# Ternary weights at the end of the first stage: the second matrix on DVE, the first on Pool

## The chip, the cores and the metric

The kernel runs on one core of a Trainium2 chip. The metric is the device time of one execution in microseconds (us). Of several runs the median is taken.

## What is computed

The reference takes `x` of 8 sequences of 512 tokens with 128 features and adds eight blocks to it in turn: a slot attention, a mixture of low-rank experts, an attention with polar positions, the experts again, a distance attention, a ternary feed-forward block, a gated attention, and the same feed-forward block again. The change touches how the two weight matrices of the feed-forward block are made. In the reference:

```
def _bitlinear(x, w_latent):
    scale = clip(mean(abs(w_latent), axis=1, keepdims=True), 1e-05, None)
    tern = clip(round(w_latent / scale), -1.0, 1.0)
    w = w_latent + (tern - w_latent)
    return x @ (w * scale).T
h = _bitlinear(x, w_fc) + gate * (x @ v.T @ fast_b.T @ u.T)
r = maximum(h, 0.0)
return _bitlinear(r * r, w_proj)
```

`w_fc` is 512x128 and `w_proj` is 128x512, both f32.

## The kernel before

The program has three groups, each a block of instruction streams for the engines, with a barrier between them: `slot_phase` (the first stage: the slot attention), `middle_group` and `last_group`. All waits between engines and within one are semaphores written by hand. Each engine's stream is the order in which the code calls the methods.

The first stage is a software pipeline over the 8 sequences b. Step s works on sequence s in its first part, s - 1 in its second, s - 2 in its third and s - 3 in the last (`batch(s, n)` gives the sequence, or none). There are 11 steps (0 to 10). In step LAST = 9 only sequence 7's third part and sequence 6's last part are left, and in step 10 sequence 7's last part. Into these two steps the class `FoldWeights` puts the preparation of weights for the later stages:

- `absolute_sums` (DVE) sums the absolute values of the rows of both matrices and signals `sums_ready`.
- `ternary(pool, i)`, i = 0 for the first matrix (fc, viewed as 4 blocks of 128x128 with a scale each) and i = 1 for the second (proj, one block of 128x512): three operations on the scales, comparisons with half the scale and its negative (lines 2293 and 2295, one for each block), a subtraction, an add and a subtraction on 128x512 (lines 2297 to 2299), and a multiply with the scale for each block (line 2301). `then_wait` makes the engine wait until an instruction of its own has finished. It works in the tiles that the trace calls `s_rzk` (fc) and `s_zk` (proj) and in `s_kT`, buffer 0. Pool does both at the end of its stream, the first matrix first, and signals `ternary_ready` after each.
- `turn_ternary(pe, i)` (line 2369) turns the four 128x128 blocks into PSUM bank 0 (fc) or 2 (proj). PE does fc in step LAST, behind `mean_squares` of sequence 7, and proj at the end of its stream, behind `project_out` of sequence 7.
- `finish_fc` (DVE, line 2375) adds the low-rank part and writes `sv.ffn1_fc`. It stands in step LAST, behind the add of sequence 6, and ahead of `apply_rms` of sequence 7. `finish_proj` (ACT, line 2379) copies the turned proj to `sv.ffn1_proj` at the end of ACT's stream.

The end of sequence 7's own work is: `mean_squares` (PE, L2177), `inverse_rms` (ACT, L2182 and L2184), `apply_rms` (DVE, L2189), `apply_gate` (DVE, L2195), `project_out` (PE, L2201, eight matmul instructions) and `add` (DVE, L2207). In the middle of the pipeline Pool's `rope` (L1884, L1889, L1890) runs beside DVE's `scan` (L1984).

Of the kernel before, what the change touches and what calls it, by code (L numbers as in the profile page):

```python
# [10 lines left out]
ALU = mybir.AluOpType  # L11
# [2198 lines left out]
class FoldWeights:  # L2210
# [4 lines left out]
    def __init__(self, nc, sv, tag, slot):  # L2215
# [15 lines left out]
        self.loaded, self.turned, self.copied, self.folded, self.kept, self.multiplied, self.products_kept, self.sums_ready, self.ternary_ready, self.ternary_turned, self.step = [  # L2231
            nc.alloc_semaphore(f"{tag}_{n}") for n in
            ("loaded", "turned", "copied", "folded", "kept", "multiplied", "products_kept", "sums_ready", "ternary_ready", "ternary_turned", "step")]
        self.steps = 0
# [37 lines left out]
    def then_wait(self, pool, instruction):  # L2272
        self.steps += 1
        instruction.then_inc(self.step, 1)
        pool.wait_ge(self.step, self.steps)
# [9 lines left out]
    def ternary(self, pool, i):  # L2285
        view, to, scale = self.raws()[i], (self.fc, self.proj)[i], self.scale[i]
        whole, low = [t.rearrange("p (k c) -> p k c", k=view.shape[1]) for t in (to, self.slot.kT[0][:, :])]
        pool.wait_ge(self.sums_ready, 2)
        self.then_wait(pool, pool.tensor_scalar(scale[1], scale[0], 1.0 / view.shape[2], 1e-5, ALU.mult, ALU.max))
        pool.tensor_scalar(scale[2], scale[1], 0.5, None, ALU.mult)  # L2290
        self.then_wait(pool, pool.tensor_scalar(scale[3], scale[1], -0.5, None, ALU.mult))
        for k in range(view.shape[1]):
            pool.tensor_scalar(whole[:, k, :], view[:, k, :], scale[2][:, k:k + 1], None, ALU.is_gt)
        for k in range(view.shape[1]):
            last = pool.tensor_scalar(low[:, k, :], view[:, k, :], scale[3][:, k:k + 1], None, ALU.is_lt)
        self.then_wait(pool, last)
        self.then_wait(pool, pool.tensor_tensor(whole, low, whole, ALU.subtract))
        self.then_wait(pool, pool.tensor_tensor(whole, whole, view, ALU.add))
        self.then_wait(pool, pool.tensor_tensor(whole, view, whole, ALU.subtract))
        for k in range(view.shape[1]):  # L2300
            last = pool.tensor_scalar(whole[:, k, :], whole[:, k, :], scale[1][:, k:k + 1], None, ALU.mult)
        last.then_inc(self.ternary_ready, 1)
# [62 lines left out]
    def turn_ternary(self, pe, i):  # L2365
        pe.wait_ge(self.ternary_ready, i + 1)
        pe.wait_ge(self.slot.a_ready[2 * i], NB)
        for k in range(NK):
            last = pe.transpose(self.banks.tensors[2 * i][:, k * P:(k + 1) * P], (self.fc, self.proj)[i][:, k * P:(k + 1) * P], self.sv.ident[:, :])
        last.then_inc(self.ternary_turned, 1)  # L2370

    def finish_fc(self, dve):
        dve.wait_ge(self.ternary_turned, 1)
        dve.wait_ge(self.products_kept, 2)
        dve.tensor_tensor(self.sv.ffn1_fc[:, :], self.banks.tensors[0][:, :], self.lowrank, ALU.add)

    def finish_proj(self, act):
        act.wait_ge(self.ternary_turned, 2)
# [3 lines left out]
def slot_phase(nc, sv, tag, a):  # L2382
# [3 lines left out]
    with nc.cleanup_on_exit():  # L2386
# [32 lines left out]
        with nc.Block() as block:  # L2419
# [16 lines left out]
            def _(pe):  # L2436
                pe.wait_ge(constants, ALL_CONSTANTS)
                pe.wait_ge(memsets, 3)
                for s in STEPS:
# [42 lines left out]
                    if s == LAST:  # L2482
                        folding.turn_ternary(pe, 0)
# [10 lines left out]
                folding.turn_ternary(pe, 1)  # L2494
# [55 lines left out]
            def _(dve):  # L2550
                slot.set_up_rows(dve)
                for s in STEPS:
# [44 lines left out]
                    if s == LAST:  # L2597
                        slot.add(dve, LAST - 3)
                        folding.finish_fc(dve)
# [10 lines left out]
                    for b in batch(s, 2):  # L2610
                        slot.apply_gate(dve, b)

            @block.gpsimd
            def _(pool):
# [18 lines left out]
                for i in range(2):  # L2633
                    folding.ternary(pool, i)
# [349 lines left out]
```

## Time and profile before

| | |
|---|---|
| runs | 1858.34, 1852.22, 1856.51 us: median 1856.51 |
| profiled execution | 1852.65 us |
| its span | 1850.9 us |
| mean granted clock of TensorE | 0.932 of full |
| busy share of PE, DVE, ACT, POOL | 87%, 66%, 70%, 20% |
| end of the first stage | about 312 us from the span's start |

The profile is of one execution. PE is TensorE's matmul, PEld its weight load, DVE is VectorE, ACT is ScalarE, POOL is GpSimd. A line number such as L2301 is that of the kernel. A tile is given with its name in the program, without its buffer number. The idle time in brackets at the end of a row is that of the engine ahead of the instruction, and behind the arrow is what ended it.

### The profile page before, as it was taken

The numbers are of one execution on the slowest core, as the hardware profiler recorded it, in microseconds if no ns is written. First come the engines' busy times: TensorE is split into PE (matmuls) and PEld (weight loads), VectorE is DVE, ScalarE is ACT, GpSimd is POOL, SyncE is SP. The second block draws the span as 40 slices with busy tenths as digits, with TensorE's granted clock in tenths as the row PEclk, the third lists the DMA queues.
The fourth block names the chain that finished last, engine by engine and source line by source line (L and its number), as shares of the span: only waits on it lengthen the run. The fifth ranks groups of instructions, "written<-read, shape, count | busy, mean of one in ns | idle before, by whom it ended". The sixth has DMA issues, their size and how long they took to land. (4 is left out here: it accounts for less than half of the span.)

```text
span 1850.9 us, 39127 instructions
## 1 busy us (share of the span) xinstructions
PE 1610.0 (87%) x14558; PEld 773.2 (42%) x14558; DVE 1227.3 (66%) x2494; ACT 1296.8 (70%) x2201; POOL 376.0 (20%) x669
## 2 busy tenths in 40 slices
PE   7999994865999999976789999777766999999988
PEld 4676763641233333345523333344441333333356
DVE  4777775798899999946410000136658999999833
ACT  4646543883788888855569999757763888888863
POOL 3423325641000000014200000023330000000153
PEclk9999896985999999998889999999975999999999
DMA  4000000055222222200132111001233222222101
GB/s 122 1 1 1 1 1 1 1 171 167 57 79 79 71 72 80 59 1 10 35 95 59 56 56 56 11 18 54 73 100 102 57 64 60 56 61 63 30 7 41
DMA packets 115392, 98.51 MB, mean 53 GB/s; under 512 B 26762, under 2 KB 105412, under 8 KB 115204
## 3 DMA queue, kind: packets, MB, share of 16 engines
q1 hardware_dynamic: 114148, 95.68, 18.2%
q8 instruction: 117, 1.92, 0.4%
q14 instruction: 71, 0.58, 0.1%
q10 hardware_dynamic: 1056, 0.33, 0.1%
HBM read 63.82 MB, written 31.59 MB: 52 GB/s over the span
## 5 line engine op out<-in xcount | busy, mean ns | idle before, releaser
L1613 ACT ACTIVATE m_probs<-m_psum 128x512 f32<-128x512 f32 (+1 forms) x768 | 513.8, 758 | 101.8 <-PE m_psum L1530 96.6
L1613 ACT ACTIVATE e_probs<-e_psum 128x512 f32<-128x512 f32 x512 | 277.2, 597 | 84.6 <-PE e_psum L1530 79.0
L1658 DVE TENSOR_REDUCE a_minus_max<-m_psum 128x1 f32<-128x512 f32 x512 | 316.2, 683 | 18.0 <-PE m_psum L1539 15.1
L1658 DVE TENSOR_REDUCE a_minus_max<-e_psum 128x1 f32<-128x512 f32 x512 | 316.1, 682 | 13.1 <-PE e_psum L1539 8.3
L1530 PE MATMUL m_psum<-m_q_stack,m_k_stack 114*32 114x512 bf16 (+1 forms) x4096 | 295.7, 385 | 17.4 <-DMA m_k_stack<-n_parts 8.4
L1550 PE MATMUL m_psum<-m_probs,m_v_ones 128*32 128x512 f32 x2048 | 270.9, 601 | 2.3 <-ACT m_probs L1613 1.6
L1530 PEld LDWEIGHTS m_psum<-m_q_stack,m_k_stack 114*32 114x32 bf16 (+1 forms) x4096 | 102.2, 96 | 222.3 <-issue 126.7
L1530 PE MATMUL e_psum<-e_q_stack,e_k_stack 126*32 126x512 bf16 x2048 | 158.5, 385 | 4.6 <-issue 2.5
L1502 POOL CAST a_max_parts<-a_minus_max 128x16 bf16<-128x16 f32 x64 | 12.6, 196 | 656.3 <-DVE a_minus_max L1658 656.3
L1550 PE MATMUL e_psum<-e_probs,e_v_ones 128*32 128x512 f32 x1024 | 133.3, 595 | 0.9 <-ACT e_probs L1613 0.8
L1539 PE MATMUL m_psum<-m_k_stack,m_q_stack 48*128 48x512 bf16 x512 | 113.4, 399 | 16.9 <-DVE a_minus_max L1658 16.7
L1603 DVE COPY m_ctxT<-m_psum 128x512 f32<-128x512 f32 x16 | 11.1, 691 | 176.4 <-PE m_psum L1550 176.4
L1539 PE MATMUL e_psum<-e_k_stack,e_q_stack 60*128 60x512 bf16 x512 | 113.4, 399 | 15.5 <-DVE a_minus_max L1658 15.3
L1530 PEld LDWEIGHTS e_psum<-e_q_stack,e_k_stack 126*32 126x32 bf16 x2048 | 43.4, 95 | 110.0 <-ACT e_probs L1613 61.7
L1550 PEld LDWEIGHTS m_psum<-m_probs,m_v_ones 128*32 128x32 f32 x2048 | 51.8, 110 | 69.0 <-ACT m_probs L1613 45.8
L1539 PEld LDWEIGHTS m_psum<-m_k_stack,m_q_stack 48*128 48x128 bf16 x512 | 29.4, 94 | 115.3 <-DVE a_minus_max L1658 86.2
L1539 PEld LDWEIGHTS e_psum<-e_k_stack,e_q_stack 60*128 60x128 bf16 x512 | 29.6, 94 | 114.8 <-DVE a_minus_max L1658 87.1
L1884 POOL TENSOR_TENSOR s_rope_product<-s_qkv,rope 128x512 f32<-128x512 f32 x32 | 40.3, 1288 | 156.4 <-ACT s_qkv L1849 156.4
L1495 POOL COPY m_v_ones<-vtok 128x128 f32<-128x128 f32 x64 | 18.6, 291 | 245.2 <-PE m_psum L1550 245.2
L254 ACT ACTIVATE e_q_stack<-x,e_v_ones 128x128 f32<-128x128 f32 x64 | 26.3, 482 | 36.2 <-POOL e_v_ones L247 36.2
L1669 DVE RECIPROCAL m_inv<-m_psum 128x32 f32<-128x32 f32 x32 | 11.3, 353 | 59.2 <-PE m_psum L1558 59.2
L2172 ACT ACTIVATE s_o<-s_bank 128x512 f32<-128x512 f32 x8 | 4.8, 597 | 58.0 <-PE s_bank L2165 58.0
(427 smaller groups left out, 2758.7 us busy)
## 6 DMA issues: line engine op xcount, KB each, us to landing
polar_q<-m_late SPq DMA_DIRECT2D x24, 256.0 KB, 3.0
polar_k<-m_late SPq DMA_DIRECT2D x24, 256.0 KB, 3.1
m_q_stack<-polar_q SPq DMA_DIRECT2D x64, 96.0 KB, 2.3
m_k_stack<-polar_k SPq DMA_DIRECT2D x64, 96.0 KB, 2.3
m_q_stack<-dist_parts SPq DMA_DIRECT2D x192, 32.0 KB
m_k_stack<-dist_parts SPq DMA_DIRECT2D x192, 32.0 KB
gate_parts<-e_late SPq DMA_DIRECT2D x24, 256.0 KB, 3.0
e_q_stack<-gate_parts SPq DMA_DIRECT2D x64, 72.0 KB
```

Of the source, the lines that this page charges most:

```text
L254: last = act.activation(self.xn[:, u, t, :], self.sv.x[:, b * NT + t, :], ACT.Identity, bias=self.shift[:, u, t:t + 1], scale=self.rstd[:, ...
L1495: pool.tensor_copy(self.buf.v_ones[n % 2][:, :, :, 16 * (n % 2):16 * (n % 2) + DH], self.sv.vtok[:, tiles_of(b), g * GW:(g + 1) * GW].rear ...
L1502: pool.tensor_copy(self.max_parts[:, 0, :], self.minus_max[n % 2][:, :]).then_inc(self.hi_ready, 1)
L1530: last = pe.matmul(self.ps_s[i % self.PAIRS][r:r + 32, j, :], self.buf.k_stack[g][0:self.rows, h, c * P + r:c * P + r + 32], self.buf.q_st ...
L1539: pe.matmul(to[:, :], self.buf.q_stack[g][part, h, t * P:(t + 1) * P], self.buf.k_stack[g][part, h, :], start=True, stop=True).then_inc(se ...
L1550: last = pe.matmul(self.ps_pv[32 * h:32 * h + self.buf.VW, :], self.buf.v_ones[m % 2][:, c, h, :], self.buf.probs[(NT * m + c) % self.buf. ...
L1603: copied = eng.tensor_copy(self.buf.ctxT[m // 2 % 2][:, :], self.ps_pv[:, :])
L1613: act.activation(self.buf.probs[(NT * m + c) % self.buf.PROBS][:, self.WIDE * part:self.WIDE * (part + 1), :], self.ps_s[i % self.PAIRS], ...
L1658: dve.tensor_reduce(self.minus_max[n % 2][:, k:k + 1], ps[:, :], AX.X, ALU.max, negate=True).then_inc(self.bank_free, 1)
L1669: dve.reciprocal(inv[:, :, :, :], raw[:, :, :, :, DH]).then_inc(self.inv_ready, 1)
L1884: pool.tensor_tensor(self.products[n][:, :, :, :], halves[:, :, :, i, :], table, ALU.mult).then_inc(self.rope_steps, 1)
L2172: act.activation(self.o2[b % 2][:, :], self.banks.of("o")[:, :], ACT.Square).then_inc(self.o2_ready, 1)
```

## The change

The work of the two ternary matrices is split over two engines. `ternary(dve, 1)` stands in DVE's stream where `finish_fc` was, in step LAST behind the add of sequence 6. Pool does `ternary(pool, 0)` alone. PE turns proj in step LAST and fc at the end of its stream. `finish_fc` goes to the end of DVE's stream. The semaphores `ternary_ready`, `ternary_turned` and `step` become one for each matrix, and the comparison's tile is `kT` buffer 0 for fc and 1 for proj.

```diff
--- before.py
+++ after.py
@@ -2228,10 +2228,11 @@
             spare[0][0:R, 0:HID], spare[0][0:R, HID:HID + D], spare[0][0:R, HID + D:HID + D + R], spare[0][:, 672:672 + D], spare[0][:, 800:800 + D])
         self.woT, self.lowrank = spare[1][:, 0:D], spare[1][:, D:D + HID]
         self.slot = slot
-        self.loaded, self.turned, self.copied, self.folded, self.kept, self.multiplied, self.products_kept, self.sums_ready, self.ternary_ready, self.ternary_turned, self.step = [
+        self.loaded, self.turned, self.copied, self.folded, self.kept, self.multiplied, self.products_kept, self.sums_ready = [
             nc.alloc_semaphore(f"{tag}_{n}") for n in
-            ("loaded", "turned", "copied", "folded", "kept", "multiplied", "products_kept", "sums_ready", "ternary_ready", "ternary_turned", "step")]
-        self.steps = 0
+            ("loaded", "turned", "copied", "folded", "kept", "multiplied", "products_kept", "sums_ready")]
+        self.ternary_ready, self.ternary_turned, self.step = [[nc.alloc_semaphore(f"{tag}_{n}{i}") for i in range(2)] for n in ("ternary_ready", "ternary_turned", "step")]
+        self.steps = [0, 0]
 
     def loads(self, a):
         sv, out = self.sv, []
@@ -2269,10 +2270,10 @@
         self.all_loaded = 16 * len(out)
         return out
 
-    def then_wait(self, pool, instruction):
-        self.steps += 1
-        instruction.then_inc(self.step, 1)
-        pool.wait_ge(self.step, self.steps)
+    def then_wait(self, eng, i, instruction):
+        self.steps[i] += 1
+        instruction.then_inc(self.step[i], 1)
+        eng.wait_ge(self.step[i], self.steps[i])
 
     def raws(self):
         return (self.sv.ffn1_fc[:, :].rearrange("p (k c) -> p k c", k=NK), self.sv.ffn1_proj[:, :, :].rearrange("p k c -> p (k c)").unsqueeze(1))
@@ -2282,24 +2283,24 @@
         for view, scale in zip(self.raws(), self.scale):
             dve.tensor_reduce(scale[0], view, AX.X, ALU.add, apply_absolute_value=True).then_inc(self.sums_ready, 1)
 
-    def ternary(self, pool, i):
+    def ternary(self, eng, i):
         view, to, scale = self.raws()[i], (self.fc, self.proj)[i], self.scale[i]
-        whole, low = [t.rearrange("p (k c) -> p k c", k=view.shape[1]) for t in (to, self.slot.kT[0][:, :])]
-        pool.wait_ge(self.sums_ready, 2)
-        self.then_wait(pool, pool.tensor_scalar(scale[1], scale[0], 1.0 / view.shape[2], 1e-5, ALU.mult, ALU.max))
-        pool.tensor_scalar(scale[2], scale[1], 0.5, None, ALU.mult)
-        self.then_wait(pool, pool.tensor_scalar(scale[3], scale[1], -0.5, None, ALU.mult))
+        whole, low = [t.rearrange("p (k c) -> p k c", k=view.shape[1]) for t in (to, self.slot.kT[i][:, :])]
+        eng.wait_ge(self.sums_ready, 2)
+        self.then_wait(eng, i, eng.tensor_scalar(scale[1], scale[0], 1.0 / view.shape[2], 1e-5, ALU.mult, ALU.max))
+        eng.tensor_scalar(scale[2], scale[1], 0.5, None, ALU.mult)
+        self.then_wait(eng, i, eng.tensor_scalar(scale[3], scale[1], -0.5, None, ALU.mult))
         for k in range(view.shape[1]):
-            pool.tensor_scalar(whole[:, k, :], view[:, k, :], scale[2][:, k:k + 1], None, ALU.is_gt)
+            eng.tensor_scalar(whole[:, k, :], view[:, k, :], scale[2][:, k:k + 1], None, ALU.is_gt)
         for k in range(view.shape[1]):
-            last = pool.tensor_scalar(low[:, k, :], view[:, k, :], scale[3][:, k:k + 1], None, ALU.is_lt)
-        self.then_wait(pool, last)
-        self.then_wait(pool, pool.tensor_tensor(whole, low, whole, ALU.subtract))
-        self.then_wait(pool, pool.tensor_tensor(whole, whole, view, ALU.add))
-        self.then_wait(pool, pool.tensor_tensor(whole, view, whole, ALU.subtract))
+            last = eng.tensor_scalar(low[:, k, :], view[:, k, :], scale[3][:, k:k + 1], None, ALU.is_lt)
+        self.then_wait(eng, i, last)
+        self.then_wait(eng, i, eng.tensor_tensor(whole, low, whole, ALU.subtract))
+        self.then_wait(eng, i, eng.tensor_tensor(whole, whole, view, ALU.add))
+        self.then_wait(eng, i, eng.tensor_tensor(whole, view, whole, ALU.subtract))
         for k in range(view.shape[1]):
-            last = pool.tensor_scalar(whole[:, k, :], whole[:, k, :], scale[1][:, k:k + 1], None, ALU.mult)
-        last.then_inc(self.ternary_ready, 1)
+            last = eng.tensor_scalar(whole[:, k, :], whole[:, k, :], scale[1][:, k:k + 1], None, ALU.mult)
+        last.then_inc(self.ternary_ready[i], 1)
 
     def turn(self, pe):
         sv, ident, bank, slot = self.sv, self.sv.ident, self.banks.tensors, self.slot
@@ -2363,19 +2364,19 @@
         act.activation(self.lowrank, bank[7][:, :], ACT.Copy, scale=sv.gate[:, 0:1]).then_inc(self.products_kept, 1)
 
     def turn_ternary(self, pe, i):
-        pe.wait_ge(self.ternary_ready, i + 1)
+        pe.wait_ge(self.ternary_ready[i], 1)
         pe.wait_ge(self.slot.a_ready[2 * i], NB)
         for k in range(NK):
             last = pe.transpose(self.banks.tensors[2 * i][:, k * P:(k + 1) * P], (self.fc, self.proj)[i][:, k * P:(k + 1) * P], self.sv.ident[:, :])
-        last.then_inc(self.ternary_turned, 1)
+        last.then_inc(self.ternary_turned[i], 1)
 
     def finish_fc(self, dve):
-        dve.wait_ge(self.ternary_turned, 1)
+        dve.wait_ge(self.ternary_turned[0], 1)
         dve.wait_ge(self.products_kept, 2)
         dve.tensor_tensor(self.sv.ffn1_fc[:, :], self.banks.tensors[0][:, :], self.lowrank, ALU.add)
 
     def finish_proj(self, act):
-        act.wait_ge(self.ternary_turned, 2)
+        act.wait_ge(self.ternary_turned[1], 1)
         act.activation(self.sv.ffn1_proj[:, :, :], self.banks.tensors[2][:, :].rearrange("p (k d) -> p k d", k=NK), ACT.Copy)
 
 
@@ -2480,7 +2481,7 @@
                     for b in batch(s, 2):
                         slot.mean_squares(pe, b)
                     if s == LAST:
-                        folding.turn_ternary(pe, 0)
+                        folding.turn_ternary(pe, 1)
                     else:
                         for b in batch(s, 3):
                             slot.project_out(pe, b)
@@ -2491,7 +2492,7 @@
                         slot.gate(pe, b)
                         slot.slot(pe, b, 1)
                         slot.slot(pe, b, 0)
-                folding.turn_ternary(pe, 1)
+                folding.turn_ternary(pe, 0)
 
             @block.scalar
             def _(act):
@@ -2596,7 +2597,7 @@
                         slot.mask_attention(dve, b, 3)
                     if s == LAST:
                         slot.add(dve, LAST - 3)
-                        folding.finish_fc(dve)
+                        folding.ternary(dve, 1)
                     for b in batch(s, 1):
                         slot.scale_logits(dve, b, 0)
                         slot.maximum(dve, b)
@@ -2609,6 +2610,7 @@
                             slot.add(dve, b)
                     for b in batch(s, 2):
                         slot.apply_gate(dve, b)
+                folding.finish_fc(dve)
 
             @block.gpsimd
             def _(pool):
@@ -2630,8 +2632,7 @@
                         slot.sum_three(pool, b)
                     for b in batch(s + 1, 0):
                         slot.rope(pool, b)
-                for i in range(2):
-                    folding.ternary(pool, i)
+                folding.ternary(pool, 0)
 
 
 _INS = []
```

## Rows read from the trace of the kernel before

**Rows 1.** The page's head.

```profile
span 1850.9 us, 39127 instructions
```

**Rows 2.** Order of time, 288 to 315 us: start, duration, engine, line, operation, tiles, idle time.

```profile
288.25 0.24 POOL L2289 TENSOR_SCALAR s_rzk<-s_rzk 128x4 f32<-128x4 f32 x1 [30.59 <-DVE s_zk L2283]
...
294.14 0.68 DVE L2207 TENSOR_TENSOR x<-s_bank,x 128x512 f32<-128x512 f32 x1
...
295.24 1.27 POOL L2298 TENSOR_TENSOR s_rzk<-s_rzk,ffn_fc 128x512 f32<-128x512 f32 x1
...
297.95 2.36 POOL L2301 TENSOR_SCALAR s_rzk<-s_rzk 128x128 f32<-128x128 f32 x4
...
299.04 0.63 ACT L2184 ACTIVATE s_o<-s_o 128x512 f32<-128x512 f32 x1
...
300.37 1.08 PE L2369 MATMUL s_bank<-ident,s_rzk 128*128 128x128 f32 x4 [2.08 <-POOL s_rzk L2301]
...
301.49 0.69 DVE L2375 TENSOR_TENSOR ffn_fc<-s_bank,s_qk 128x512 f32<-128x512 f32 x1 [6.67 <-PE s_bank L2369]
...
302.10 0.68 DVE L2189 TENSOR_TENSOR s_og<-s_bank,s_o 128x512 f32<-128x512 f32 x1
...
302.81 0.69 DVE L2195 TENSOR_TENSOR s_og<-s_og,s_sig 128x512 f32<-128x512 f32 x1
...
303.56 2.08 PE L2201 MATMUL s_bank<-slot_wo,s_og 128*128 128x128 f32 x8 [2.10 <-DVE s_og L2195]
...
305.67 0.69 DVE L2207 TENSOR_TENSOR x<-s_bank,x 128x512 f32<-128x512 f32 x1 [2.17 <-PE s_bank L2201]
...
308.99 1.57 POOL L2301 TENSOR_SCALAR s_zk<-s_zk 128x512 f32<-128x512 f32 x1
...
310.62 1.11 PE L2369 MATMUL s_bank<-ident,s_zk 128*128 128x128 f32 x4 [4.99 <-POOL s_zk L2301]
...
311.77 0.60 ACT L2379 ACTIVATE ffn_proj<-s_bank 128x512 f32<-128x512 f32 x1 [12.10 <-PE s_bank L2369]
...
314.26 0.87 DVE L228 BATCH_NORM_STATS2 m_ctxT<-x 128x6 f32<-128x128 f32 x4 [7.90 <-PEq L2386]
```

**Rows 3.** The view of waits, 284 to 315 us: total, times, longest.

```profile
DVE ffn_fc L2375 <- PE s_bank L2369: 6.7, 1, 6.7
```

**Rows 4.** DVE's instructions of two lines (ns min/median/max), and a group of the page.

```profile
L568 DVE TENSOR_SCALAR m_late<-pope_table,m_late x1: 481/481/481, 317.4 to 317.4; 128x512 f32<-128x512 f32 x1
...
L559 DVE TENSOR_SCALAR m_late<-m_late x1: 153/153/153, 315.6 to 315.6; 128x1 f32<-128x1 f32 x1
...
L1905 DVE TENSOR_SCALAR vtok<-s_bank 128x512 f32<-128x512 f32 x32 | 21.7, 681 | 20.1 <-PE s_bank L1895 20.1
```

**Rows 5.** Order of time, 217.5 to 221.2 us; L1984's instructions (ns min/median/max).

```profile
217.57 1.27 POOL L1889 TENSOR_TENSOR s_qk<-s_rope_product 128x512 f32<-128x512 f32 x1
...
217.78 2.14 DVE L1984 TENSOR_TENSOR_SCAN s_zvT<-ones,s_wvT 128x512 f32<-128x512 f32 x1
...
218.81 2.18 POOL L1890 TENSOR_TENSOR s_qk<-s_rope_product 128x512 f32<-128x512 f32 x1
...
L1984 DVE TENSOR_TENSOR_SCAN s_zvT<-ones,s_wvT x16: 1212/1224/2167, 42.1 to 280.3; 128x512 f32<-128x512 f32 x16
```

**Rows 6.** Order of time at 302.77; L2290's instructions (ns min/median/max).

```profile
302.77 2.10 POOL L2295 TENSOR_SCALAR s_kT<-ffn_proj,s_zk 128x512 f32<-128x512 f32 x1
...
L2290 POOL TENSOR_SCALAR s_rzk<-s_rzk x1: 405/405/405, 288.6 to 288.6; 128x4 f32<-128x4 f32 x1
...
L2290 POOL TENSOR_SCALAR s_zk<-s_zk x1: 211/211/211, 300.7 to 300.7; 128x1 f32<-128x1 f32 x1
```

**Rows 7.** Busy time by stretch: PE, PEld, DVE, ACT, POOL, PEclk, DMA share, GB/s.

```profile
300.00:302.00 2.00, 1.08 (x4) 0.68 (x4) 0.51 (x1) 0.00 (x0) 1.73 (x5) 0.61 0.00 0
302.00:326.00 24.00, 7.99 (x33) 6.80 (x34) 11.68 (x58) 8.01 (x17) 14.80 (x21) 0.50 0.00 1
326.00:328.00 2.00, 2.00 (x13) 2.00 (x13) 1.63 (x9) 1.59 (x5) 1.92 (x4) 0.56 0.00 0
```

## The prediction

> **What bounds the kernel now.** I read the page first: 1850.9 us of span on one core [rows 1]. The change touches only the end of the first stage, so I went to the order of time there and looked for what ends last [rows 2]. The stage ends at a barrier, and the next stage's first DVE instruction comes at 314.26. Three chains run into that barrier. Pool makes the ternary weights of the first matrix (fc) from 288.25 to 300.31 (297.95 plus 2.36), then those of the second (proj) until 310.56 (308.99 plus 1.57). PE turns proj from 310.62 to 311.73 and ACT copies it from 311.77 to 312.37: this is the last work of the stage. The second chain is sequence 7 through DVE and PE (`apply_rms`, `apply_gate`, `project_out`, `add`), which ends at 306.36 (305.67 plus 0.69). The third, `finish_fc`, is in the middle of the second: DVE has waited 6.67 us for it and starts it at 301.49. The view of waits says the same of DVE: 6.7 us for fc [rows 3]; ACT has waited 12.10 us for proj [rows 2]. So the stage's end is set by Pool's serial 22.3 us, and DVE has idle time from 294.82 to 301.49. From ACT's end to the next stage's first DVE instruction is 1.89 us, which I leave as it is.
>
> **What the change does to each chain.** Nothing before 294.82 moves: the sums that both need are ready at 288.2, and DVE reaches the place of `ternary(dve, 1)` with the end of the add of sequence 6 (294.14 plus 0.68). Pool's queue loses proj (10.25 us, 310.56 less 300.31) and nothing is queued behind it. The transposes and ACT's copy of proj keep their size, only their time changes. No DMA is issued or moved.
>
> DVE's new work is nine instructions: three on one column, two comparisons, three two-input operations and one multiply, each on 128x512 f32. The nearest DVE rows: 0.153 us for a column [rows 4], 0.48 for a tensor_scalar from SBUF to SBUF (0.48 is the row; the same form from PSUM takes 0.68, and I keep that as the upper bound), 0.69 for a two-input operation with both inputs in SBUF (302.81) [rows 2, 4]. Alone that is 0.5 + 3 x 0.48 + 3 x 0.69 plus some 0.04 per dependency, about 4.2 us, so DVE would be ready at 299.1; with the upper bound for the tensor_scalars, at 299.7.
>
> But it isn't alone, because Pool is at fc at the same time. The trace shows that the two exclude each other. A DVE scan with two SBUF inputs began at 217.78, 0.21 us into a Pool operation that ran to 218.84, and took 2.14 us, where its like takes 1.22; it ended at 219.92, 1.08 after Pool's end. Pool's next operation began at 218.81 and took 2.18 instead of 1.27; it ended at 220.99, 1.07 after DVE's end [rows 5]. So each waited for the other's whole operation, and turns were taken. From this an operation holds the common resource for its time less 0.14 (DVE) or 0.20 (Pool). Pool's proj comparison shows it again: 2.10 us where the like multiply takes 1.57 [rows 2, 6], with DVE's 0.69 us two-input operation in it: 0.53 lost, as 0.69 less 0.14 would have it. For DVE's tensor_scalar the witness is Pool's four-column operation that took 405 ns beside it and 211 ns otherwise [rows 6].
>
> The Trainium skill, SBUF — State Buffer, section Who interferes with whom, says that DVE in a two-port mode, or with two SBUF inputs, and a GpSimd operation lock each other out for the whole instruction, and that the one that issues first wins. By that rule this change puts two engines on one port and would give little beyond taking turns; the trace agrees where it shows it (2.14 us against 1.22). Without any lock the sum would be the 7.5 us below.
>
> The walk by turns, from 294.8. DVE's three columns are done and its first comparison begins at about 295.2, as Pool's subtraction ends; it holds to 295.5. Pool's add (295.24 in the trace) then holds 1.07, to 296.6; DVE's second comparison to 296.8; Pool's second subtraction to 297.9; DVE's subtraction (0.54) to 298.45; then Pool's four multiplies, 0.40 of hold each, alternate with DVE's add (0.54), subtraction (0.54) and multiply (0.27): 298.85, 299.4, 299.8, 300.3, 300.7, 301.0, and Pool's last to 301.4. So DVE has proj at about 301.1 (2.0 later than alone) and Pool has fc at 301.5 (1.2 later than 300.31).
>
> From there: ACT's inverse rms has been ready since 299.67 (299.04 plus 0.63), so `apply_rms` starts at 301.1 in place of 302.10, `apply_gate` at 301.85 in place of 302.81, and PE starts `project_out` at 302.6 in place of 303.56. PE turns proj before that: 1.08 us from 301.2 to 302.3, in the gap; ACT copies it by 303.0. What is queued behind PE's wait for DVE's proj is `project_out` alone, and its own input comes later from the same DVE queue, so that wait costs nothing. `project_out` ends at 304.7 (2.08). Behind it PE turns fc, which has been ready since 301.5: four transposes at the low clock's 0.22 each, to 305.55. DVE adds sequence 7 from 304.7 to 305.4, then `finish_fc` (0.69) from 305.6 to 306.3. That is the new end: 312.37 less 306.3, **6.1 us less**. What is late next is no longer Pool but DVE's and PE's chain of sequence 7, with the turn of fc and `finish_fc` appended (0.9 us).
>
> `finish_fc` moved to the end costs 0.9 there; in its old place it held up sequence 7 by 6.67 us. The three more semaphores and the barrier I price at nothing: their cover is the 1.89 us between stages; were it gone, some tenths.
>
> **Rivals.**
> *Pool wins every turn.* Its steps follow each other within 0.1 us, so DVE might get in only when Pool is through. Then fc is ready at 300.6, DVE does a subtraction, an add, a subtraction and the multiply after it (0.54 + 0.72 + 0.72 + 0.5, about 2.5) and is at `apply_rms` at 303.1, 1.0 later than in the trace; `project_out` runs 304.6 to 306.7, the turn of fc to 307.5, the end is 308.2. Gain 4.2 us, 0.23%. For it: the back-to-back Pool steps. Against: the scan did get in between two of them [rows 5].
> *No contention worth the name.* DVE is ready at 299.1 to 299.7 and waits for the rms (299.67); `project_out` 301.1 to 303.2, fc turned by 304.1, end 304.9. Gain 7.5 us, 0.40%. Against it the same rows. If instead DVE wins every turn, it is through at 299.1, Pool at about 303.8, fc is turned by 304.9 and the end is 305.7: 6.7 us, near my own.
> *The gain is given back later.* The next stage starts 6 us earlier against PE's clock, which fell at 301 (0.61 in 300 to 302) and rose at 327 (0.56 in 326 to 328) [rows 7]. If it rises no earlier than now, 6 us more of that stage's PE work is done at 1.2 GHz. Those 6 us hold at most 3 us of PE work at full speed that would take 6, and DVE and ACT share the path, so I estimate 1 to 3 us given back, leaving 3 to 5: within 0.3%.
> *Slower.* The same clock is the mechanism: the place is the second stage's head, the price is one us for each us of fully busy PE work that falls from 2.4 to 1.2 GHz. The sign turns at 6.1 us of such work, and slower by 0.3% (5.6 us) needs 11.7 us of it. Between 326 and 328 PE is fully busy, so it isn't impossible, but from 302 to 326 PE is busy 7.99 of 24 us [rows 7], a third, so it would take a far longer low stretch to hold 11.7 us of PE work. Time: 1862.
> *The change doesn't do what it says*, that is, DVE's ternary isn't started in its idle time: it can't be late, as its inputs are ready 6 us before.
>
> **How the numbers follow.** The sum is made against the profiled execution: 1850.9 of span and 1852.65 in all, so 1844.8 and 1846.6 there; the median of the runs shown is 1856.51, 3.9 above the profiled one, and the same 6.1 us from it give 1850.4 (0.33%). Chances: turns taken, or DVE first (6.1 to 6.7 us), 0.45; Pool first 0.15; no contention 0.15; part given back 0.19; slower 0.06. A measurement of this kernel can tell about 0.3% (5.6 us) from nothing; the three runs lie 6.1 us apart. My forecast stands just past that bound, so two thirds of its chance count as faster, with nine tenths of no contention and some tenth of the others: 0.48. Slower 0.06, within 0.3% the rest, 0.46. The range: no contention gives 1849, Pool first 1852, given back 1851.5 to 1853.5; with the scatter of a median of such runs, 2 to 3 us each way, 1846 to 1857.
>
> **What the profile after would show.** DVE's nine instructions from 294.8 to about 301, some with 1.3 to 1.6 us where 0.69 is normal; Pool's steps of fc stretched likewise and done at 301 to 302; `project_out` of sequence 7 at about 302.6; DVE's `finish_fc` last, at about 305.6 to 306.3; the next stage's first DVE instruction at about 308.2. Wrong would be: a comparison on DVE well over 0.68 with Pool idle; Pool's fc later than 304.7, when it, and no longer sequence 7, would set the end; a barrier longer than 1.9 us; or the rest of the kernel taking over 1 us more than its present 1536.6 us from 314.26 to the end.

## The result and the profile after

The change makes the kernel a little faster, by 0.38%. Over 20 runs each, the median goes from 1855.20 us (1851.39 to 1863.30) to 1847.71 us (1844.27 to 1856.48); the ratio is 0.9962, with a 95% interval of 0.9947 to 0.9976, which is 4.4 to 9.8 us. The forecast was 1850.4 in a range of 1846 to 1857, and 6.1 us of gain. The profiled execution takes 1846.34 us, its span is 1844.6, 6.3 less than before.

Order of time at the end of the changed kernel's first stage, the counterpart of [rows 2]:

```profile
289.25 0.24 POOL L2290 TENSOR_SCALAR s_rzk<-s_rzk 128x4 f32<-128x4 f32 x1 [30.59 <-DVE s_zk L2284]
...
295.05 0.68 DVE L2207 TENSOR_TENSOR x<-s_bank,x 128x512 f32<-128x512 f32 x1
...
295.89 0.14 DVE L2292 TENSOR_SCALAR s_zk<-s_zk 128x1 f32<-128x1 f32 x1
...
296.07 0.48 DVE L2294 TENSOR_SCALAR s_zk<-ffn_proj,s_zk 128x512 f32<-128x512 f32 x1
...
296.25 1.43 POOL L2299 TENSOR_TENSOR s_rzk<-s_rzk,ffn_fc 128x512 f32<-128x512 f32 x1
...
296.47 1.50 DVE L2296 TENSOR_SCALAR s_kT<-ffn_proj,s_zk 128x512 f32<-128x512 f32 x1
...
297.76 1.33 POOL L2300 TENSOR_TENSOR s_rzk<-ffn_fc,s_rzk 128x512 f32<-128x512 f32 x1
...
298.00 1.64 DVE L2298 TENSOR_TENSOR s_zk<-s_kT,s_zk 128x512 f32<-128x512 f32 x1
...
299.19 3.24 POOL L2302 TENSOR_SCALAR s_rzk<-s_rzk 128x128 f32<-128x128 f32 x4
...
299.67 0.74 DVE L2299 TENSOR_TENSOR s_zk<-s_zk,ffn_proj 128x512 f32<-128x512 f32 x1
...
299.94 0.63 ACT L2184 ACTIVATE s_o<-s_o 128x512 f32<-128x512 f32 x1
...
301.62 0.68 DVE L2189 TENSOR_TENSOR s_og<-s_bank,s_o 128x512 f32<-128x512 f32 x1
...
301.76 1.11 PE L2370 MATMUL s_bank<-ident,s_zk 128*128 128x128 f32 x4 [2.58 <-DVE s_zk L2302]
...
303.09 2.08 PE L2201 MATMUL s_bank<-slot_wo,s_og 128*128 128x128 f32 x8 [0.21 <-DVE s_og L2195]
...
306.06 0.69 DVE L2376 TENSOR_TENSOR ffn_fc<-s_bank,s_qk 128x512 f32<-128x512 f32 x1 [0.16 <-PE s_bank L2370]
...
308.30 0.87 DVE L228 BATCH_NORM_STATS2 m_ctxT<-x 128x6 f32<-128x128 f32 x4 [1.55 <-PEq L2387]
```

The line numbers are one higher than before. All times of the stage are counted here from Pool's first instruction on the first matrix (fc), 289.25 in this trace and 288.25 before: it is released by DVE's second sum, and nothing ahead of it differs between the kernels. (This trace reached that point 1.00 us later than the one before.)

- DVE does its nine instructions from 295.64 to 301.71. The first comparison takes 0.48. The second takes 1.50 and the subtraction 1.64: each stands beside one of Pool's (296.25, 297.76).
- Pool has fc at 302.43 (299.19 plus 3.24), 13.18 from the start of the count, against 12.06 before. Its four multiplies take 3.24 where they took 2.36 [rows 2].
- `apply_rms` starts at 301.62, 1.05 after its input from ACT's `inverse_rms` ("the rms" from here on) is ready (299.94 plus 0.63); it began 2.43 after it before. PE has turned the second matrix (proj) in the gap (301.76); `project_out`, the turn of fc and `finish_fc` follow. The wait of 6.67 us in front of `finish_fc` [rows 2, 3] has shrunk to fractions.
- The last work ends at 306.75, 17.50 from the start of the count; before it was 312.37, 24.12. The next stage's first DVE instruction comes at 308.30, 19.05, against 26.01 [rows 2].

So the end of the stage is 6.62 us sooner, and the barrier behind it is 0.34 shorter (1.55 against 1.89): 6.96. The rest, from the next stage's start to the end, is 1536.3 us against 1536.6 before. With the 1.00 us of later start: 1.00 less 6.96 less 0.34 is the 6.30 of the span.

TensorE's clock in the changed kernel, the counterpart of [rows 7] (stretch, then PE, PEld, DVE, ACT, POOL, PEclk, DMA share, GB/s):

```profile
300.00:302.00 2.00, 0.23 (x1) 0.24 (x2) 1.93 (x4) 0.57 (x1) 2.00 (x4) 0.81 0.00 0
320.00:322.00 2.00, 2.00 (x13) 2.00 (x13) 1.59 (x9) 1.63 (x5) 1.90 (x4) 0.57 0.00 0
```

The rise from 1.2 to 2.4 GHz, which came in 326 to 328 before (0.56), comes in 320 to 322 now (0.57): it moved along with the stage. The clock fell in 300 to 302 in both kernels (0.61 before, 0.81 now), ahead of `project_out`, which took 2.08 us in both.

### The profile page after: what moved, and what is told of

It reads as the page before. It is cut to its first block and busy times, and to the rows that moved or that the text cites. A ratio compares the mean times of both kernels' runs of the same rounds, so it can differ in the third digit from the quotient of the medians.

```text
span 1844.6 us, 39127 instructions
## 1 busy us (share of the span) xinstructions
PE 1611.5 (87%) x14558; PEld 774.0 (42%) x14558; DVE 1231.9 (67%) x2503; ACT 1296.9 (70%) x2201; POOL 367.9 (20%) x660
## 3 DMA queue, kind: packets, MB, share of 16 engines
q1 hardware_dynamic: 114148, 95.68, 18.3%
```

## The experiments

Two points are used for all of them: where the stage's last work ends, counted from Pool's first instruction on fc (in e6 on proj; where Pool does none, from 0.09 us after DVE's second sum, the gap of the others), and the ratio of the runs to the kernel before. The ratio of the change is from the 20 runs above, each experiment's from 12 runs beside runs of the kernel before, with its 95% interval.

| kernel | stage ends at | ratio to before |
|---|---|---|
| before | 24.12 | 1 |
| the change | 17.50 | 0.9962 (0.9947 to 0.9976) |
| e1 order alone | 24.11 | 1.0004 (0.9990 to 1.0019) |
| e2 split alone | 19.89 | 0.9993 (0.9974 to 1.0011) |
| e8 split alone, again | 19.79 | 0.9978 (0.9958 to 0.9997) |
| e3 Pool's fc left out | 15.34 | 0.9963 (0.9948 to 0.9978) |
| e4 first half early | 17.19 | 0.9960 (0.9942 to 0.9978) |
| e5 fc turned first | 17.84 | 0.9965 (0.9947 to 0.9984) |
| e6 matrices swapped | 18.54 | 0.9986 (0.9969 to 1.0002) |
| e7 all on DVE | 19.78 | 0.9985 (0.9968 to 1.0002) |
| e9 split further | 17.91 | 0.9964 (0.9949 to 0.9980) |
| e10 the change, again | 17.47 | 0.9966 (0.9951 to 0.9980) |

Each stage end is from one profile. They can be compared to about 0.1 us where PE's clock was the same (17.50 and 17.47), or where Pool's work and not sequence 7's attention sets the end (24.12 and 24.11; 19.89 and 19.79), and not elsewhere. In e1, e3, e4, e5, e7 and e9 `project_out` ran at 2.4 GHz and took 1.16 us instead of 2.08. In e2, e4, e5 and e9 some of sequence 7's attention ran at 1.2 GHz, which made the rms late.

### e1: the order alone

```diff
                         slot.add(dve, LAST - 3)
-                        folding.finish_fc(dve)
...
                         slot.apply_gate(dve, b)
+                folding.finish_fc(dve)
```

> Pool makes both matrices as before; only finish_fc goes to the end of DVE's stream. My theory (Pool's serial 22 us set the end of the stage): sequence 7 runs some 2 us earlier, but Pool still has the second matrix ready 16.4 us after DVE's start of the add of sequence 6, and ACT's copy still ends 18.2 us after it. No change: within 0.3 us in the profile. Rival (it was the 6.67 us in which finish_fc held up DVE that set the end): the stage ends 2 us or more sooner.

```profile
287.79 0.24 POOL L2289 TENSOR_SCALAR s_rzk<-s_rzk 128x4 f32<-128x4 f32 x1 [32.60 <-DVE s_zk L2283]
...
299.50 0.69 DVE L2189 TENSOR_TENSOR s_og<-s_bank,s_o 128x512 f32<-128x512 f32 x1 [4.88 <-ACT s_o L2184]
...
300.31 0.68 POOL L2290 TENSOR_SCALAR s_zk<-s_zk 128x1 f32<-128x1 f32 x1
...
302.77 0.68 DVE L2375 TENSOR_TENSOR ffn_fc<-s_bank,s_qk 128x512 f32<-128x512 f32 x1
...
308.52 1.57 POOL L2301 TENSOR_SCALAR s_zk<-s_zk 128x512 f32<-128x512 f32 x1
...
311.30 0.60 ACT L2379 ACTIVATE ffn_proj<-s_bank 128x512 f32<-128x512 f32 x1 [11.84 <-PE s_bank L2369]
...
313.79 0.87 DVE L228 BATCH_NORM_STATS2 m_ctxT<-x 128x6 f32<-128x128 f32 x4 [10.34 <-PEq L2386]
```

`apply_rms` starts at 299.50, as soon as the rms is there, and DVE is done with everything at 303.45. It changes nothing: Pool has proj at 310.09, and ACT's copy ends at 311.90, 24.11 from the start of the count, against 24.12. The ratio says the same. That DVE was held up for 6.67 us was true, and cost nothing, because Pool's two matrices in a row set the end.

### e2 and e8: the split alone

```diff
                         folding.ternary(dve, 1)
+                        folding.finish_fc(dve)
...
                     if s == LAST:
-                        folding.turn_ternary(pe, 1)
+                        folding.turn_ternary(pe, 0)
...
-                folding.turn_ternary(pe, 0)
+                folding.turn_ternary(pe, 1)
...
-                folding.finish_fc(dve)
```

> DVE makes the second matrix, Pool the first, but finish_fc stays ahead of apply_rms and PE turns the first matrix in step LAST, the second at the end. My theory: DVE waits for Pool's first matrix (7.4 us after the start of the add of sequence 6), its turn and finish_fc, then sequence 7 follows; the last work is ACT's copy, about 14.3 us after that start, against 18.2 before and 11.7 with the whole change. Gain 3.9 us (0.21%), the order then being worth 2.6. Rival (the split alone carries the gain): it ends within 0.5 us of the whole change, at 11.7.

> The same kernel as e2_split_alone, once more, since the stage ended 4.6 us sooner but the median of its runs fell by only 1.3 to 3. If the stage's gain reaches the whole time: ratio 0.9975 (0.996 to 0.999). If it is given back later: ratio 0.999 to 1.000 again.

The second run's trace:

```profile
291.12 0.24 POOL L2290 TENSOR_SCALAR s_rzk<-s_rzk 128x4 f32<-128x4 f32 x1 [32.69 <-DVE s_zk L2284]
...
304.12 1.11 PE L2370 MATMUL s_bank<-ident,s_rzk 128*128 128x128 f32 x4 [2.67 <-POOL s_rzk L2302]
...
305.27 0.69 DVE L2376 TENSOR_TENSOR ffn_fc<-s_bank,s_qk 128x512 f32<-128x512 f32 x1 [1.35 <-PE s_bank L2370]
...
310.31 0.60 ACT L2380 ACTIVATE ffn_proj<-s_bank 128x512 f32<-128x512 f32 x1 [7.47 <-PE s_bank L2370]
...
312.44 0.87 DVE L228 BATCH_NORM_STATS2 m_ctxT<-x 128x6 f32<-128x128 f32 x4 [2.29 <-PEq L2387]
```

Sequence 7 waits for Pool's fc, its turn (304.12) and `finish_fc` (305.27), and the end is at 310.91, 19.79 from the start of the count; 19.89 in e2. So the split alone takes 4.3 us off the stage and the order, worth nothing by itself, another 2.3 on top of it (expected 3.9 and 2.6). The count from the add of sequence 6, which the expectation used, turned out a poor one: in e2 it gives 12.76 and in e8 13.60, since PE's clock moves that add. The ratios, 0.9993 and 0.9978, hold the expected 0.9975 in both intervals, and in both they hold 0.999 as well, the value that was expected if the gain is given back.

The traces show that a part of it was. From the next stage's first DVE instruction to the last group's first one it is 879.4 us in the kernel before, 881.0 in e2 and 881.5 in e8: 1.7 and 2.1 us more. In the kernel before PE's clock rises 12 to 14 us after that first instruction, in e2 16 to 18 and in e8 18 to 20 us after it. A late rise doesn't always cost as much: in e3 it came as late as in e8, and the stretch took 879.4.

### e3: without Pool's work on fc

```diff
+        if i == 0:
+            eng.memset(to, 0.0).then_inc(self.ternary_ready[0], 1)
+            return
```

> The whole change, but Pool leaves out the ternary of the first matrix: one memset of zeros stands in its place, so the first matrix keeps only its low-rank part. Lock theory (DVE's two slow instructions waited for Pool's whole operations): DVE's second comparison goes from 1.50 to 0.48 us and its subtraction from 1.64 to 0.69 to 0.74, DVE is done with the second matrix 4.8 us after the start of the add of sequence 6 instead of 6.66, apply_rms then waits for ACT's rms (5.5 us after it), and the stage ends at about 10.6 to 10.8 instead of 11.7: gain over the change 0.9 to 1.1 us. Rival (the 1.50 and 1.64 are the price of these operations on DVE with its own dependencies): they stay, and the end stays at 11.7.

```profile
295.08 0.68 DVE L2207 TENSOR_TENSOR x<-s_bank,x 128x512 f32<-128x512 f32 x1
...
296.51 0.48 DVE L2299 TENSOR_SCALAR s_kT<-ffn_proj,s_zk 128x512 f32<-128x512 f32 x1
...
297.03 0.69 DVE L2301 TENSOR_TENSOR s_zk<-s_kT,s_zk 128x512 f32<-128x512 f32 x1
...
299.21 0.48 DVE L2305 TENSOR_SCALAR s_zk<-s_zk 128x512 f32<-128x512 f32 x1
...
300.64 0.69 DVE L2189 TENSOR_TENSOR s_og<-s_bank,s_o 128x512 f32<-128x512 f32 x1 [0.95 <-ACT s_o L2184]
...
302.12 1.16 PE L2201 MATMUL s_bank<-slot_wo,s_og 128*128 128x128 f32 x8 [1.71 <-DVE s_og L2195]
...
303.92 0.68 DVE L2379 TENSOR_TENSOR ffn_fc<-s_bank,s_qk 128x512 f32<-128x512 f32 x1
```

The second comparison is back at 0.48 and the subtraction at 0.69; DVE is done at 299.69, 4.61 after the start of the add of sequence 6 (295.08), against 6.66 in the changed kernel. `apply_rms` now waits 0.95 for the rms. The lock theory (each engine waits for the other's operation) holds: being together with Pool costs DVE 2.05 us, and sequence 7's chain 1.01 of it (`apply_rms` 5.56 after that add instead of 6.57). The stage's end at 15.34 overstates it, because `project_out` took 1.16 here: with the 5.13 us that the changed kernel takes from the start of `apply_rms` to the end, it would be 16.51, an estimate.

The price depends on where DVE's start falls among Pool's operations. The nine instructions take 4.0 us alone (e3), 5.2 in e2 and e5, 6.0 in e8 and 6.1 in the changed kernel. In e2 and e5 only the second comparison is held up (1.50), because Pool is at its four short multiplies from DVE's subtraction on.

### e4: the first half of DVE's work earlier

```diff
                         folding.keep(dve)
+                        folding.ternary(dve, 1)
...
-                        folding.ternary(dve, 1)
+                        folding.ternary_end(dve, 1)
```

`ternary` ends behind the first subtraction here and `ternary_end` is the rest, on Pool too.

> The whole change, but DVE does the scales, the two comparisons and the first subtraction of the second matrix right after keep, in the 2.7 us in which it waited for sequence 7's attention, and only the add, the subtraction and the multiply in the later place. My theory: sequence 7's chain is no longer held up by DVE; apply_rms starts when the rms is ready (5.5 us after the start of the add of sequence 6), the stage ends at about 10.8 instead of 11.7: 7.4 us less than before. Rival (turns with Pool's eight comparisons stretch the early half beyond the gap): mask_attention of sequence 7 starts up to 1 us late, the whole chain shifts by that, and the gain stays at 6 to 6.5 us.

```profile
291.60 0.73 DVE L2298 TENSOR_TENSOR s_zk<-s_kT,s_zk 128x512 f32<-128x512 f32 x1
...
293.56 2.48 DVE L2149 TENSOR_TENSOR s_a_masked<-s_bank,causal 128x512 f32<-128x512 f32 x4 [1.22 <-PE s_bank L2142]
...
302.85 0.69 DVE L2189 TENSOR_TENSOR s_og<-s_bank,s_o 128x512 f32<-128x512 f32 x1 [2.17 <-ACT s_o L2184]
```

The early half ends at 292.33 and `mask_attention` at 293.56 waits for PE, not for DVE: it fits into the gap, and the rival is out. It was Pool that paid: its first four comparisons took 2.88 us instead of 2.36 beside it. Later DVE waits 2.17 us for the rms, so DVE is off the chain as expected. The stage's end of 17.19 isn't the expected gain all the same: the rms came 1.9 us later from the start of the count than in the changed kernel (13.20 against 11.32), as PE did sequence 7's matmuls in part at 1.2 GHz, and `project_out` 0.92 shorter. What the stage would gain with the same clock this run doesn't show.

### e5: fc turned ahead of `project_out`

```diff
                         folding.turn_ternary(pe, 1)
+                        folding.turn_ternary(pe, 0)
...
                         slot.apply_gate(dve, b)
-                folding.finish_fc(dve)
+                    if s == LAST:
+                        folding.finish_fc(dve)
```

> The whole change, but PE turns the first matrix ahead of project_out of sequence 7, and finish_fc stands between apply_gate and the add of sequence 7. Times from Pool's first instruction of the first matrix (17.5 us to the end of the stage with the change, 24.1 before). My theory: Pool has the first matrix at 13.2, its turn takes 1.1 at the low clock, project_out starts at 14.3 instead of 13.8, finish_fc is hidden behind it, the stage ends with the add of sequence 7 at 17.1: 0.4 sooner. Rival: each wait for Pool put into sequence 7's chain costs more than the turn behind it; the end is at 17.8 or later.

```profile
303.93 0.69 DVE L2189 TENSOR_TENSOR s_og<-s_bank,s_o 128x512 f32<-128x512 f32 x1 [1.59 <-ACT s_o L2184]
...
305.27 0.68 DVE L2376 TENSOR_TENSOR ffn_fc<-s_bank,s_qk 128x512 f32<-128x512 f32 x1
...
306.60 0.69 DVE L2207 TENSOR_TENSOR x<-s_bank,x 128x512 f32<-128x512 f32 x1 [0.65 <-PE s_bank L2201]
```

`finish_fc` is hidden under `project_out`, and the stage ends with the add: 3.36 us from the start of `apply_rms`. The changed kernel takes 5.13, but at the other clock; e3 and e4, which have the changed kernel's order and `project_out` at 1.16 as here, take 3.96. So the tail is 0.60 shorter. But the rms was 3.13 us late by PE's clock and came after Pool's fc, so the case that the rival speaks of, a wait for Pool in sequence 7's chain, did not arise. The end of 17.84 settles neither.

### e6: the matrices swapped

```diff
-                        folding.ternary(dve, 1)
+                        folding.ternary(dve, 0)
...
-                folding.ternary(pool, 0)
+                folding.ternary(pool, 1)
```

with PE's two turns swapped back to fc first.

> DVE makes the first matrix (18 instructions, four to a step) and Pool the second (9), all else as with the change: the DVE one is turned first, the Pool one last. My theory (a split of either kind takes 10 us off Pool's queue and fits DVE's gap): DVE needs 0.6 us more than for the second matrix, Pool is done 2 us sooner, the stage ends at 18.0 to 18.3 (from Pool's first instruction) against 17.5 with the change and 24.1 before. Rival (four small instructions take turns with Pool four times as often): DVE takes over 9 us where it took 6.1, and the end is beyond 20.

```profile
296.05 0.16 DVE L2290 TENSOR_SCALAR s_rzk<-s_rzk 128x4 f32<-128x4 f32 x1
...
296.11 1.28 POOL L2300 TENSOR_TENSOR s_zk<-ffn_proj,s_zk 128x512 f32<-128x512 f32 x1
...
296.24 1.17 DVE L2291 TENSOR_SCALAR s_rzk<-s_rzk 128x4 f32<-128x4 f32 x1
...
302.04 0.87 DVE L2302 TENSOR_SCALAR s_rzk<-s_rzk 128x128 f32<-128x128 f32 x4
...
307.26 0.60 ACT L2380 ACTIVATE ffn_proj<-s_bank 128x512 f32<-128x512 f32 x1 [6.29 <-PE s_bank L2370]
```

DVE needs 6.86 us (296.05 to 302.91) for fc, against 6.07 for proj: 0.8 more, where 0.6 was expected, although it has 18 instructions for 9. The end is 18.54, a little over the expected 18.0 to 18.3 and far from 20. Of the 1.04 over the changed kernel 0.33 are PE's: its clock rose later, and the add of sequence 6 started 6.13 from the start of the count instead of 5.80. So which matrix goes to which engine is worth some 0.7 us, while the two engines and the order together are worth 5.6 even this way round.

### e7: all on DVE

```diff
                         slot.apply_gate(dve, b)
+                    if s == LAST:
+                        folding.ternary(dve, 0)
...
-                folding.ternary(pool, 0)
```

> DVE makes both matrices, the second in the place of the change and the first behind apply_gate of sequence 7; Pool none. My theory: no instruction is stretched (comparison 0.48, subtraction 0.69), apply_rms starts when the rms is ready, the first matrix takes DVE 4.5 to 5.3 us from then, and the stage ends about 19.5 us after the DVE sums are ready (17.5 with the change, 24.1 before): a gain over before of 4.5, so that Pool's share with all its taking of turns is worth 2. Rival (the common port makes Pool's share worthless): the end is at 17.5 or sooner.

```profile
302.28 0.16 DVE L2290 TENSOR_SCALAR s_rzk<-s_rzk 128x4 f32<-128x4 f32 x1
...
306.62 0.87 DVE L2302 TENSOR_SCALAR s_rzk<-s_rzk 128x128 f32<-128x128 f32 x4
...
308.70 0.69 DVE L2376 TENSOR_TENSOR ffn_fc<-s_bank,s_qk 128x512 f32<-128x512 f32 x1 [0.61 <-PE s_bank L2370]
```

Nothing is stretched, fc takes DVE 5.21 us (302.28 to 307.49), and the end is at 19.78 (19.5 expected). Against DVE alone in this order, Pool's share is therefore worth 2.3 us, although Pool needs over twice DVE's time for it and takes 2.05 from DVE. Another order of DVE's work, with a part of it in the gap that e4 uses, might do better without Pool; it was not tested.

### e9 and e10: a further split, and the change once more

e9 gives DVE's wait for sequence 7's attention more to do, and takes over e5's order:

```diff
                         folding.keep(dve)
+                        folding.scales(dve)
+                        folding.below(dve, 0).then_inc(folding.early, 1)
+                        folding.above(dve, 1)
...
-                        folding.ternary(dve, 1)
+                        folding.then_wait(dve, 1, folding.below(dve, 1))
+                        folding.combine(dve, 1)
...
-                folding.ternary(pool, 0)
+                pool.wait_ge(folding.early, 1)
+                folding.then_wait(pool, 0, folding.above(pool, 0))
+                pool.wait_ge(folding.early, 2)
+                folding.combine(pool, 0)
```

`above` and `below` are the comparisons with plus and minus half the scale, `combine` the rest of `ternary`.

> A further split. DVE uses its wait for sequence 7's attention for all scales, the four negative comparisons of the first matrix and the first comparison of the second; Pool makes the rest of the first matrix, DVE the rest of the second in the later place; PE turns both matrices ahead of project_out and finish_fc stands between apply_gate and the add of sequence 7. Times from the end of DVE's second sum (plus 0.1), as in the other runs. My theory: Pool has the first matrix at about 11, DVE the second at about 11.5, both are turned by 13.2, and the stage ends with the add of sequence 7 at 16.0 at the low clock (17.5 with the change, 24.1 before). Rival (the early comparisons don't fit): mask_attention starts over 0.5 us after PE's attention is done, and the end is at 17 or later. In the runs' median the 1.5 us are 0.08% and can't be seen beside the change.

> The changed kernel itself once more, beside e9 on the same chip: ratio 0.9962 again (0.995 to 0.9975), the stage ending at 17.5 where TensorE's clock is as it was, and up to 2 us later or 1 sooner where it isn't.

```profile
293.04 2.48 DVE L2149 TENSOR_TENSOR s_a_masked<-s_bank,causal 128x512 f32<-128x512 f32 x4 [2.10 <-PE s_bank L2142]
...
299.17 0.49 DVE L2320 TENSOR_SCALAR s_zk<-s_zk 128x512 f32<-128x512 f32 x1
...
302.87 0.69 DVE L2189 TENSOR_TENSOR s_og<-s_bank,s_o 128x512 f32<-128x512 f32 x1 [3.22 <-ACT s_o L2184]
...
305.54 0.69 DVE L2207 TENSOR_TENSOR x<-s_bank,x 128x512 f32<-128x512 f32 x1 [0.65 <-PE s_bank L2201]
```

DVE has proj at 299.66 and Pool fc at 299.79, 11.34 and 11.47 from the start of the count (11.5 and 11 expected); `mask_attention` starts 0.05 after PE. DVE then waits 3.22 us for the rms, which PE's low clock made late again, so the end is 17.91 and not 16.0. From the rms to the end it is 3.40 us, against 6.18 in the changed kernel (5.01 with `project_out` at 1.16: the wait of 1.05 and the 3.96 of e3 and e4): the stage's end is now set by sequence 7 alone. In the runs e9 and the change, on one chip, can't be told apart: 0.9964 and 0.9966. In this profile the clock rose 18 to 20 us after the next stage's first DVE instruction, and the stretch from there to the last group took 883.3 us instead of the changed kernel's 879.2: 4.1 us lost behind the stage.

e10 is the changed kernel. Its stage ends at 17.47, and yet its span is 1851.6 us, 7.0 more than that of the first profile of the same kernel. Of these, 6.4 lie in the head of the last group, from its first DVE instruction to its first attention activation. That stretch in the first profile of the changed kernel:

```profile
1187.50:1419.60 232.10, 161.77 (x682) 90.70 (x682) 132.73 (x280) 133.27 (x230) 65.86 (x93) 0.83 0.24 69
```

in the second:

```profile
1188.00:1426.50 238.50, 169.18 (x682) 94.52 (x682) 130.39 (x280) 133.85 (x229) 65.00 (x93) 0.80 0.23 67
```

in the kernel before:

```profile
1193.60:1425.90 232.30, 161.71 (x682) 90.86 (x682) 132.88 (x280) 133.22 (x230) 65.79 (x93) 0.83 0.24 69
```

and in e1:

```profile
1194.00:1433.00 239.00, 169.20 (x682) 94.56 (x682) 130.43 (x280) 133.93 (x230) 65.07 (x93) 0.79 0.23 67
```

The same 682 PE instructions take 161.8 us of PE time at a mean clock of 0.83, or 169.2 at 0.80 and 0.79, and the stretch 232.1 to 232.3 us or 238.5 to 239.0, in either kernel alike. Over the 20 runs of the changed kernel, the time and the mean granted clock go together with a correlation of -0.95: 1.16 us more for each 0.001 less (a least-squares line through the time and clock of each run; the clocks go from 0.922 to 0.933).

## Why the prediction was right

Step by step, with the walk's times turned to the count from Pool's first instruction:

- **Pool's serial work set the end, not the wait in DVE.** Shown by e1 (24.11) beside e2 and e8 (19.89 and 19.79).
- **Turns at a common resource.** Shown by e3: 1.50 and 1.64 go back to 0.48 and 0.69. The prediction's walk by turns had DVE's second comparison and its subtraction each wait for a whole Pool operation, and they did. It was off in the small: the add and the subtraction beside Pool's short multiplies took 0.74 instead of the 0.95 of taking turns, so DVE was done at 12.46, not 12.85: 0.48 sooner by these, less 0.09 by which its first subtraction ended later than in the walk. Pool lost 1.12 us (13.18 against 12.06; 1.2 expected). The rival in which Pool wins every turn is refuted, and so is that of no contention. The stage's 6.62 us lie near the 6.7 of the case in which DVE wins every turn, but that had DVE done at 10.85: DVE won only against the short multiplies. One witness was misread: the 211 ns of [rows 6] are of a one-column operation, and not of the four-column one. It stands all the same, because in e6 a one-column operation in that place took 0.41 too.
- **From DVE's multiply on.** `project_out` at 13.84 (14.35 expected), the end at 17.50 (18.05 expected). The 0.55 are DVE's 0.39 and small gaps; the order of events is the one forecast.
- **PE's clock at `project_out`: luck.** The forecast took over 2.08 us from the trace before, and both profiles of the changed kernel have it. Nothing in the walk made sure of it: in six of the experiments it was 1.16, and with the tail of 3.96 of e3 and e4 the end would be 16.33.
- **The barrier priced at nothing.** It gave 0.34 us, which the forecast lacked.
- **Nothing given back later.** From the next stage's first DVE instruction to the last group's first one it is 879.2 and 879.6 us in the two profiles of the changed kernel, against 879.4 before, and the clock's rise moved along. The prediction had no reason for that beyond its chance of 0.19, and e2, e8 and e9 show that it can go otherwise. That the whole rest agreed to 0.3 us (1536.3 against 1536.6) is luck: it was 1543.2 in e10, the same kernel, because the last group's clock was lower, and by the prediction's own sign of being wrong (over 1 us more) that profile would have counted against it.

Together 6.96 us against the 6.07 of the sum (24.12 less 18.05): the mis-sized terms are DVE's work beside Pool (0.39), the barrier (0.34) and gaps (0.16), all on the same side. The median came out 2.7 us below the 1850.4 of the forecast: 0.9 are these terms, 1.3 are the base (the three runs' median, 1856.51, where that of 20 is 1855.20), and the rest is scatter. The rule of the Trainium skill, SBUF — State Buffer, section Who interferes with whom, agrees with e3; that the one that comes second waits for the whole of the other is what the 1.50 and 1.64 show, though beside Pool's 0.6 us multiplies DVE hardly waited and Pool paid nearly all (3.24 against 2.36).

Of the chance of 0.46 for no visible change, about 0.15 was scatter around the forecast itself and 0.3 belonged to the two rivals that the traces refute for this kernel, Pool first and the gain given back. The forecast of a visible change was close all the same: the ratio's interval, 0.9947 to 0.9976, lies beyond 0.3% in its middle and not with its upper end.

## What to carry to other kernels

A long wait in one engine's stream is worth nothing to remove while another engine's chain ends later: here it was worth 0.0 us alone and 2.3 once the longer chain was cut. Two engines that exclude each other at SBUF can still be worth splitting work over, if one of them was idle: the collision held sequence 7's chain up by 1 us, while the split and the order took 6.6 off the stage. Where a change is local, count from an event that nothing in the change moves: the stage repeated to 0.03 us between two profiles whose spans differed by 7.0. Such a count repeats only where PE's clock does, so the clock's rows belong beside it, and so does the stretch behind the change.

## What the runs showed of the hardware

- **The price on Pool and on DVE.** The same nine steps on proj take Pool 10.2 us in the kernel before (300.40 to 310.56, with 0.53 lost to DVE in it) and DVE, alone, 4.0 (e3, 295.68 to 299.69): 1.57 against 0.48 for a tensor_scalar, 1.27 against 0.69 for a two-input operation.
- **DVE's one-column operations weren't held up, a four-column one was.** DVE's 128x1 operations took 0.14 to 0.15 in the middle of a Pool operation (295.89 in the changed kernel), while the one 128x4 operation that began inside a Pool operation, in e6 (296.24, Pool's from 296.11 to 297.39), took 1.17 instead of 0.16. Pool's own one-column operation has no such exemption: in e1 it took 0.68 (300.31) instead of 0.21 beside DVE's two-input `apply_gate`.
- **The barrier is longer behind Pool.** From the last work to the next stage's first DVE instruction it is 1.89 us in the kernel before and in e1, where Pool's last instruction ends 1.81 before ACT's, and 1.53 to 1.57 in the changed kernel and in e2 to e8, whichever of ACT and DVE is last. In both of the former it is 3.70 from Pool's last instruction. e2 and e8 end with the same turn and copy as the kernel before, but Pool is done early there, and it is 1.53. That Pool takes so long to arrive is the likely reason; it was not tested by itself.
- **The spread of the runs goes with PE's clock.** The same kernel's profiles differ by 6.4 us in one stretch of 232, with the clock at 0.83 or 0.80.
